# Layer norm moments by VectorE's aggregation, with epsilon and sign on GpSimd, in a fused macaron block

## The reference

```python
def _layernorm(x, axis=-1, eps=1e-05):
    m = jnp.mean(x, axis=axis, keepdims=True)
    v = jnp.var(x, axis=axis, keepdims=True)
    return (x - m) / jnp.sqrt(v + eps)

x = x + 0.5 * ffn(_layernorm(x), ...)
x = x + attn(_layernorm(x), ...)
x = x + 0.5 * ffn(_layernorm(x), ...)
```

## Time and profile before

| | us |
|---|---|
| median of 3 runs | 1548.77 |
| lowest, highest | 1546.59, 1553.33 |
| profiled execution, whole | 1546.01 |
| profiled execution, span of the trace | 1544.1 |
| mean granted TensorE clock in the span | 0.994 |

### The profile page before, as it was taken

The page is one execution under the profiler, slowest core; times in us unless marked ns, Lnnn a source line. Parts: engine busy times, 40 slices in busy tenths (PEclk is TensorE's granted clock), DMA queues, the critical chain, the costliest instruction groups (busy, mean ns, idle before and its releaser), DMA issues.

```text
span 1544.1 us, 19065 instructions
## 1 busy us (share of the span) xinstructions
PE 1478.7 (96%) x6914; PEld 1207.3 (78%) x6914; DVE 1079.0 (70%) x1477; ACT 681.5 (44%) x1066; POOL 555.4 (36%) x402
## 2 busy tenths in 40 slices
PE   6999999999999999999999989999999999989998
PEld 5787877777778787878787768887877787778887
DVE  7536787867887777868876868696868788952322
ACT  7653444353535344435353435353544435433442
POOL 3021434270544353424452253606252608080110
PEclk9999999999999999999999999999999999999999
DMA  9567577766585756856767658574757676843332
GB/s 364 206 248 236 180 251 254 249 220 209 194 294 203 261 195 223 295 188 220 258 203 247 219 188 284 182 274 162 250 187 247 225 266 207 304 136 133 119 110 69
DMA packets 188065, 338.19 MB, mean 219 GB/s; under 512 B 15424, under 2 KB 138432, under 8 KB 187584
## 3 DMA queue, kind: packets, MB, share of 16 engines
q1 hardware_dynamic: 187968, 336.93, 63.7%
HBM read 314.85 MB, written 30.41 MB: 224 GB/s over the span
## 4 chain that ended last, share of the span: by engine, by line
PE 70%; DVE 12%; POOL 6%; ACT 5%; DMA 4%; issue 3%; SPq 1%; DVEq 0%; POOLq 0%; ACTq 0%
PE f_bank L1144 23%; PE f_bank L1145 23%; PE a_banks L1222 7%; PE f_bank L1092 5%; PE f_bank L1093 4%; PE f_bank L1173 2%; DVE slot L1003 2%; PE f_bank L1174 2%; POOL acc L741 2%; PE a_banks L1242 2%; DVE S L1009 2%; DVE slot L1047 2%; POOL acc L738 2%; DMA slot<-keys_and_values 1%; DVE h_lo L906 1%
## 5 line engine op out<-in xcount | busy, mean ns | idle before, releaser
L1144 PE MATMUL f_bank<-h_hi,wring 128*128 128x512 f32 x2048 | 808.6, 395 | 4.3 <-DMA wring<-weights_hi 1.7
L1145 PE MATMUL f_bank<-h_lo,wring 128*128 128x512 f32 x2048 | 798.4, 390 | 0.0
L1144 PEld LDWEIGHTS f_bank<-h_hi,wring 128*128 128x128 f32 x2048 | 385.0, 188 | 88.8 <-issue 4.5
L1145 PEld LDWEIGHTS f_bank<-h_lo,wring 128*128 128x128 f32 x2048 | 384.9, 188 | 80.3 <-issue 1.4
L824 ACT ACTIVATE h_hi<-f_bank,colv 128x512 fp32r<-128x512 f32 x256 | 176.3, 689 | 502.1 <-PE f_bank L1145 501.8
L906 DVE TENSOR_TENSOR h_lo<-f_bank,h_hi 128x512 fp32r<-128x512 f32 x256 | 175.1, 687 | 218.4 <-ACT f_bank L825 217.6
L755 POOL TENSOR_TENSOR h_lo<-f_gated,h_hi 128x512 fp32r<-128x512 f32 x128 | 168.1, 1325 | 383.1 <-ACT h_hi L818 382.0
L1092 PE MATMUL f_bank<-fT_hi,w_in 128*128 128x512 f32 x512 | 209.4, 409 | 22.4 <-DVE f_gated L915 12.5
L1093 PE MATMUL f_bank<-fT_lo,w_in 128*128 128x512 f32 x512 | 202.6, 396 | 0.0
L1047 DVE TENSOR_TENSOR slot<-slot,a_banks 128x1280 f32<-128x1280 f32 (+4 forms) x124 | 169.6, 1376 | 13.0 <-DMA slot<-keys_and_values 12.9
L1009 DVE TENSOR_REDUCE S<-slot 128x80 f32<-128x1280 f32 (+4 forms) x124 | 171.7, 1385 | 4.3
(11 more groups left out here) (123 smaller groups left out, 1275.0 us busy)
## 6 DMA issues: line engine op xcount, KB each, us to landing
wring<-weights_hi SPq DMA_DIRECT2D x248, 512.0 KB, 4.8
slot<-keys_and_values SPq DMA_DIRECT2D x128, 384.0 KB, 4.6
slot<-keys_and_values SPq DMA_DIRECT2D x64, 640.0 KB, 3.9
slot<-keys_and_values SPq DMA_DIRECT2D x312, 128.0 KB, 4.5
slot<-keys_and_values SPq DMA_DIRECT2D x64, 256.0 KB, 5.1
weights_hi<-in_ffn_w SPq DMA_DIRECT2D x16, 512.0 KB, 6.8
keys_and_values<-kv_out SPq DMA_DIRECT2D x32, 256.0 KB, 2.5
slot<-in_ffn_w SPq DMA_DIRECT2D x10, 512.0 KB, 6.9
```

What stands on the lines that cost most here:

```text
L1144: pe.matmul(bank[:, :], hi, h_hi[src][:, k, :], start=(k == 0), stop=False)
L1145: last = pe.matmul(bank[:, :], hi, h_lo[src][:, k, :], start=False, stop=(not general and k == KH - 1))
```

## The change

`moments` and its seven instructions go. In their place VectorE runs one aggregation instruction for each block of statistics, 4 for an FFN tile and 2 for an attention sub-tile; it writes mean and variance side by side. GpSimd now waits for these, multiplies the mean by -1 and adds epsilon to the variance in two instructions, waits for itself, and goes on as before. Two semaphores of each norm become one. The planned places change too: among `TIMES` those of `q`, `kv1` and `out`, in `FOLLOW` that of `lo`, among `STARTS` those of sub-tiles 11 and 12.

```diff
@@ -29,14 +29,14 @@
 
 STEPS = ["stats", "turn", "kv0", "q", "kv1", "gate", "score", "score step", "ahead", "max", "weigh", "weigh step",
          "z", "out"]
-TIMES = [4.03, 9.45, 11.2, 13.1, 17.5, 26.66, 22, 3.95, 6.75, 53.01, 60.41, 3.2, 94.86, 3.17]
+TIMES = [4.03, 9.45, 11.2, 13.54, 18.01, 26.66, 22, 3.95, 6.75, 53.01, 60.41, 3.2, 94.86, 3.53]
 
 FOLLOW = dict(silu=-1.5, gate=0.1, cut=2.12, low=2.21, gelu=-1.01,
-              lo=0.9, residual=-1.57, residual2=-0.2, fill=23.38, stats=-1.02, turn=4)
+              lo=1.7, residual=-1.57, residual2=-0.2, fill=23.38, stats=-1.02, turn=4)
 
 OPENING = dict(block=6.5, block_step=1.84, compare=1.3, turn=8.7, input=13.0, count=52.85)
 STARTS = [41.0, 114.5, 182.4, 268.3, 337.6, 405.3, 485.5, 567.2,
-          636.9, 716.8, 782.1, 866.5, 947.5, 1023.3, 1099.1, 1163.8]
+          636.9, 716.8, 782.1, 864.5, 946.9, 1023.3, 1099.1, 1163.8]
 
 
 class Counts:
@@ -225,16 +225,17 @@
         S = sb("S", [P, SB, HEADS, NU])
         merge = sb("merge", [P, 3, HEADS, NT])
         a_st = sb("a_st", [P, SB, 6])
-        a_mo = sb("a_mo", [P, 5, SB])
-        a_mean = sb("a_mean", [P, SB])
+
+        a_mv = sb("a_mv", [P, SB, 2])
+        a_less_mean = sb("a_less_mean", [P, SB])
         a_shift = sb("a_shift", [P, SB])
         a_var = sb("a_var", [P, SB])
         a_rs = sb("a_rs", [P, SB])
         mx = sb("mx", [P, SB, HEADS])
         sm = sb("sm", [P, SB, HEADS])
         f_st = sb("f_st", [P, NB, 6])
-        f_mo = sb("f_mo", [P, 5, NB])
-        f_mean = sb("f_mean", [P, NB])
+        f_mv = sb("f_mv", [P, NB, 2])
+        f_less_mean = sb("f_less_mean", [P, NB])
         f_shift = sb("f_shift", [P, NB])
         f_var = sb("f_var", [P, NB])
         f_rs = sb("f_rs", [P, NB])
...
@@ -705,17 +706,21 @@
             pool.wait_ge(s_neg, 1)
             pool.memset(acc[:, 0, :], 0.0).then_inc(s_zero, 1)
 
+            def scale_and_shift(run, mv, less_mean, var, rs, shift, moments, vareps, power, rstd):
+
+                pool.wait_ge(moments, run.at(1, 1))
+                pool.tensor_scalar(less_mean[:, :], mv[:, :, 0], -1.0, None, ALU.mult)
+                pool.tensor_scalar(var[:, :], mv[:, :, 1], EPS, None, ALU.add).then_inc(vareps, 1)
+                pool.wait_ge(vareps, run.at(1, 1))
+                pool.tensor_tensor(rs[:, :], var[:, :], half_neg[:, 0:rs.shape[1]], ALU.pow).then_inc(power, 1)
+                pool.wait_ge(power, run.at(1, 1))
+                pool.tensor_tensor(shift[:, :], less_mean[:, :], rs[:, :], ALU.mult).then_inc(rstd, 1)
+
             def f_rstd_(r):
-                pool.wait_ge(f_vareps, r.at(1, 1))
-                pool.tensor_tensor(f_rs[:, :], f_var[:, :], half_neg[:, :], ALU.pow).then_inc(f_pow, 1)
-                pool.wait_ge(f_pow, r.at(1, 1))
-                pool.tensor_tensor(f_shift[:, :], f_mean[:, :], f_rs[:, :], ALU.mult).then_inc(f_rstd, 1)
+                scale_and_shift(r, f_mv, f_less_mean, f_var, f_rs, f_shift, f_moments, f_vareps, f_pow, f_rstd)
 
             def a_rstd_(a):
-                pool.wait_ge(a_vareps, a.at(1, 1))
-                pool.tensor_tensor(a_rs[:, :], a_var[:, :], half_neg[:, 0:SB], ALU.pow).then_inc(a_pow, 1)
-                pool.wait_ge(a_pow, a.at(1, 1))
-                pool.tensor_tensor(a_shift[:, :], a_mean[:, :], a_rs[:, :], ALU.mult).then_inc(a_rstd, 1)
+                scale_and_shift(a, a_mv, a_less_mean, a_var, a_rs, a_shift, a_moments, a_vareps, a_pow, a_rstd)
 
             def a_bout_(a):
                 rows_ = xa[:, a.u, :, :]
@@ -855,27 +860,15 @@
 
         @block.vector
         def _(dve):
-            def moments(run, st, mo, mean, var, stats, summed, squared, vareps):
-
-                even, odd = (1, 2), (4, 5)
-                dve.wait_ge(stats, run.at(1, 1))
-                dve.tensor_tensor(mo[:, 0, :], st[:, :, even[0]], st[:, :, odd[0]], ALU.add)
-                dve.tensor_tensor(mo[:, 1, :], st[:, :, even[0]], st[:, :, odd[0]], ALU.subtract)
-                dve.tensor_tensor(mo[:, 2, :], st[:, :, even[1]], st[:, :, odd[1]], ALU.add).then_inc(summed, 1)
-                dve.wait_ge(summed, run.at(1, 1))
-                dve.tensor_scalar(mean[:, :], mo[:, 0, :], -0.5, None, ALU.mult)
-                dve.tensor_tensor(mo[:, 3, :], mo[:, 1, :], mo[:, 1, :], ALU.mult)
-                dve.tensor_scalar(mo[:, 4, :], mo[:, 2, :], 1.0 / D, EPS, ALU.mult, ALU.add).then_inc(squared, 1)
-                dve.wait_ge(squared, run.at(1, 1))
-                dve.scalar_tensor_tensor(var[:, :], mo[:, 3, :], 0.25, mo[:, 4, :], ALU.mult, ALU.add)\
-                    .then_inc(vareps, 1)
-
             def f_stats_(r):
                 dve.wait_ge(f_loaded[r.p], r.j // 2 * 16 + 16)
                 for n in range(NB):
                     last = dve.bn_stats(f_st[:, n, :], xf[:, r.p, n, :])
                 last.then_inc(f_stats, 1)
-                moments(r, f_st, f_mo, f_mean, f_var, f_stats, f_summed, f_squared, f_vareps)
+                dve.wait_ge(f_stats, r.at(1, 1))
+                for n in range(NB):
+                    last = dve.bn_aggr(f_mv[:, n, :], f_st[:, n, :])
+                last.then_inc(f_moments, 1)
 
             def f_tlo_(r, bp):
                 dve.wait_ge(f_thi, r.at(2, bp + 1))
@@ -978,7 +971,10 @@
                 for n in range(SB):
                     last = dve.bn_stats(a_st[:, n, :], xa[:, u, n, :])
                 last.then_inc(a_stats, 1)
-                moments(a, a_st, a_mo, a_mean, a_var, a_stats, a_summed, a_squared, a_vareps)
+                dve.wait_ge(a_stats, a.at(1, 1))
+                for n in range(SB):
+                    last = dve.bn_aggr(a_mv[:, n, :], a_st[:, n, :])
+                last.then_inc(a_moments, 1)
 
             def a_evict(a, what):
                 dve.wait_ge(a_proj, a.at(4, PROJECTIONS.index(what) + 1))
```

More of the change, by code:

```diff
@@ L288, in macaron_kernel @@
         f_stored = [sem(f"f_stored{i}") for i in range(2)]
-        f_stats, f_summed, f_squared = sem("f_stats"), sem("f_summed"), sem("f_squared")
+        f_stats, f_moments = sem("f_stats"), sem("f_moments")
         f_vareps, f_pow, f_rstd = sem("f_vareps"), sem("f_pow"), sem("f_rstd")
@@ L297, in macaron_kernel @@
         a_stored = [sem(f"a_stored{i}") for i in range(2)]
-        a_stats, a_summed, a_squared = sem("a_stats"), sem("a_summed"), sem("a_squared")
+        a_stats, a_moments = sem("a_stats"), sem("a_moments")
         a_vareps, a_pow, a_rstd = sem("a_vareps"), sem("a_pow"), sem("a_rstd")
```

## The result

The kernel after took 1544.36 us (median of 16 runs, 1541.23 to 1546.59), the kernel before on the same chip 1549.1 us (16 runs, 1546.59 to 1554.35). The ratio is 0.9966 with a 95% interval of 0.9955 to 0.9976: 5.3 us less, between 3.7 and 7.0. The forecast was 1540 in a range of 1529 to 1551. The profiled execution took 1541.23 us, 4.8 less than that of before.

What follows compares the result with a forecast made beforehand. TensorE was taken as the bound, busy 1478.7 of 1544.1 us, so only its waits could go. Operations -7.35 and places -1.5 gave -8.9 us: 1537.1 from the profiled execution, 1548.8 by the median shown, forecast 1540, range 1529 to 1551.

Steps and rivals of the forecast that it cites:

- rival 2: In the norms, GpSimd holds the aggregation as it held the sums: 1548 us, chance 0.17.
- The waits for `h_lo`: TensorE's three waits behind held statistics go, -4.0 us, and the one at 1144 us, -1.0.
- The step at 1062 us: TensorE's stop for `h_lo` there goes, and the half clock after it: -3.7 us together.
- The 885 us place: The 4.2 us wait for a product goes, but GpSimd then decides through `a_hat`: -0.6 us.
- GpSimd's addition: Two small instructions ahead of each norm's power, 0.16 us each with a turn of 0.08: +0.4 us an episode.
- `a_hat` at 664 us: GpSimd runs without pause to the power there, so its new instructions make the wait longer: +0.4 us.
- The clock: Without the stop at 1062 us, TensorE's matmuls behind it no longer run at half clock: -1.4 us.
- The places: New planned order of the engines' steps, all over the kernel: together -1.5 us, bounds +6 and -7.
- The gain at 1352 us: Two weighings pass an `h_lo`, starting GpSimd's chain of the last sub-tile earlier: -0.8 us.
- `fT_lo` passing an `h_lo`: On VectorE, the later of the pair ends as before and TensorE needs both only after the second turn: 0.
- Rival 1: Freed VectorE time and new places pay more, through GpSimd's chains and gate products: another 7 us, 1533, chance 0.27.
- Rival 3: GpSimd becomes the bound of the norm, deciding from +1.7 us an episode: 1557 us, chance 0.09 with a late `h_lo`.

Runs made afterwards that it cites:

- reduce_dve: Kernel after, with sign and epsilon moved from GpSimd to two one-input reductions on VectorE: 1537.63 us, ratio 0.9932 to the kernel before.
- places_only: Kernel before with only the new planned places, the seven operations kept: 1546.22 us, ratio 0.9983 to the kernel before.
- agg_only: Kernel after with the planned places of the kernel before: 1544.15 us, ratio 0.9959 to the kernel before.
- one_held: Kernel after with one unused two-input VectorE addition ahead of each norm's aggregations: 1547.1 us, ratio 0.9995 to the kernel before.
- reduce_old_places: Kernel after with sign and epsilon as two VectorE reductions and the planned places of the kernel before: 1538.66 us, ratio 0.9928 to the kernel before.
- power_first: Kernel after with VectorE's first comparison waiting for GpSimd's first power: 1543.66 us, ratio 0.996 to the kernel before.
- pool_more: Kernel after with two more small, unused GpSimd instructions per norm: 1551.34 us, ratio 1.0016 to the kernel before.
- no_eps: Kernel after without the GpSimd addition of epsilon and its semaphore turn: 1539.04 us, ratio 0.9928 to the kernel before.

## Why the prediction was right, and where it was off

**The hold on the aggregation (rival 2).** It runs free: 96 times at most 0.183 us. But the reason I gave, one input from SBUF, is not enough, and a row of the kernel before could have told me: the multiplication L866 has one input too and took up to 2.878 us. It started 11 times with a GpSimd instruction running and was held each time. The aggregation, the statistics and the reductions of reduce_dve (64, the longest 0.158 us) are free, the two-input operations and that multiplication are not. The multiplication with an addition, L868, says nothing: it stands right behind the two-input L867 and never met a GpSimd instruction with more than 0.4 us left. The Trainium skill (Advanced Engine Details and Errata, VectorE Performance Modes) lists the multiplication's kind of instruction with a mode that uses both ports and the reduction without one, and has no line for the aggregation; by its list the traces agree, while its trigger by place and even counts alone would have held the aggregation.

**The waits for `h_lo`.** All four are gone. The step at 1062 us came out to a tenth (-3.7 with its half clock). But places_only takes that stop away too, with the sums still held, so this number agrees with the mechanism and does not prove it. That holds cost time is shown by agg_only (-4.1 at full clock) and one_held (3.1 back).

**The 885 us place.** The mechanism was as walked: the wait for the product turned into one for `a_hat`. The gain is 0.27 us instead of 0.6, since GpSimd's addition is 0.60 us and not 0.4.

**GpSimd's addition** is the step that was mis-sized: two instructions that I took at 0.16 us each take 0.23 and start 0.30 apart. The 0.2 us of difference looks like nothing, but at 8 us of the kernel for each us it is 1.6 us, and I had walked only the norms with a visible wait. Two that showed none before, at 1222 and 1292 us, have one of 0.88 and 0.28 now, and so has the FFN norm at 652 us (0.79). The whole addition of 0.60 us costs 4.8 us (agg_only against reduce_old_places); without it freeing VectorE was worth 8.9 us at full clock, and half went back. The forecast counted 1 to 2 for it. The trace shows why a norm without a hold gains nothing: from the end of its statistics to the end of its shift the quickest attention norm takes 1.94 us before and 1.96 after, the quickest FFN norm 2.27 and 2.43. In reduce_old_places they take 1.59 and 2.04.

**`a_hat` at 664 us** is luck. The +0.4 came, but from the FFN norm at 652 us, which the forecast did not walk; the wait for `a_hat` itself fell by 0.16.

**The clock.** I booked -1.4 us for the half clock behind 1062 us. It is gone there, but the time at half clock up to TensorE's last matmul, 17 us in the profiled execution before, is 17 us after too: another stretch of 3.4 us came at 80 us. Over all runs, span times the missing part of the clock is 12.4 us after and 11.0 to 12.4 us before, by chip. The term was right as a place and nothing as a sum.

**The opening** was not in the sum. GpSimd's first power came to lie behind VectorE's comparison. It cost 1.26 us at the first transposes in the profiled execution. That the whole opening was 3.5 us longer is one execution's number: agg_only's first attention norm starts at 108.93 us, before's at 109.17, after's at 112.65. The rest of after's delay is the wait for weights at 77 us (2.42 us against 1.23) and the half clock behind it. power_first, which mends the power, still has 112.55: its transposes are 0.4 us later than before's, by 30 us it is 1.9 us behind, its wait for weights is 0.47, and a wait of 2.04 us for the `h_lo` that the new places put behind `fT_lo` (at 84 us) and a half clock behind it make up the rest. Why after waits longer for weights is open.

**The places.** Forecast -1.5. By the ratio -2.6 alone, at full clock -0.9. The gain at 1352 us (-0.8) came at 1379 us as -0.2 of the wait, -0.5 in the ledger. The forecast put nothing on `fT_lo` passing an `h_lo`, since TensorE would need both only after the second turn. That was wrong at 82 us: 1.21 us in places_only, against 0.18 before.

**Rival 1** was half right: gate products did gain, 12.5 to 6.9 us, of which 4.2 is only the place at 885 us. **Rival 3** has the right mechanism. Its point of decision was too high: I put it at +1.7 us a norm, and pool_more is already slower than before (1.0004 to 1.0028) at +0.60 +0.40 = 1.0 us.

## What to carry to other kernels

Small operations on a few numbers are dear where they meet GpSimd: ask for each instruction on VectorE whether it can be held until a running GpSimd instruction ends, and choose a form that can't (here statistics, aggregation, reduction). When work is moved to free an engine with slack, price the latency of the chain first: here the small operations off VectorE gained 8.9 us at full clock where GpSimd got nothing more to do, and 0.60 us on GpSimd in each norm took half of it back. Where two versions lie within a few us, compare their times at full clock beside the medians, since what half clock took from the span differed by up to 2.7 us between kernels. And where a stop goes away, look whether it goes in the kernel with only the order changed: a stop that depends on what happens to meet there proves little.

## What the runs showed that was not expected

- GpSimd can be held as well as VectorE. A GpSimd power of 4 numbers took 2.13 us instead of 1.04 (after), and the product behind it 1.24 instead of 0.24 (power_first), beside one two-input VectorE instruction of 1.23 us. The Trainium skill (SBUF — State Buffer, SBUF: two separate sides) says that whichever of the two starts first has the pair of ports for its whole instruction. The held sums and these two agree. A power that starts first does not: in the kernel before it runs from 7.15 to 8.17 us, the comparison starts at 7.28 and still takes 1.23; in agg_only they start at 7.21 and 7.24, and the comparison takes 1.25.
- A one-input multiplication on VectorE is held (up to 2.88 us for 2 numbers), a one-input reduction is not (0.15 us).
- A GpSimd multiplication or addition on 2 or 4 numbers is busy for 0.23 us. Of the chain it costs 0.20 us each where two more stand in a row (pool_more), and 0.42 where a semaphore turn goes with it (no_eps).
- Unheld VectorE time isn't free at 66% busy: 29.3 us of it behind the norms cost 4.8 us, 0.16 us for each us.
